# Fewer GpSimd additions in the last attention head, a later place in the queue for the first expert's weights, and a projection bias that GpSimd adds at the layer's start

## The reference

```
x = x + conv_attn(group_norm(x))      # 12 heads of 32 channels, 1024 x 1024 scores, with row and column biases by relative position
t = t + attn(layer_norm(t))           # 12 heads of 32 channels, the same 1024 tokens, plain scores
t = t + experts(layer_norm(t))        # 8 experts (384 -> 1536 -> 384), each token goes to its two best ones
# in each attention layer:
attn = softmax(q @ k.T * scale)       # per head
out  = (attn @ v) @ w_proj.T + b_proj
```

## Time and profile before

| | us |
|---|---|
| median of 3 runs | 1007.57 |
| the runs | 1009.1, 1007.57, 1000.21 |
| profiled execution, its time | 1002.1 |
| profiled execution, its span | 1000.3 |

### The profile page before, as it was taken

One profiled execution on the slowest core, in us unless ns is written; L12 is line 12 of the kernel. 1 busy time (PEld: TensorE's weight loads), 2 busy tenths in 40 slices (PEclk: granted clock), 3 DMA queues, 4 the chain that ended last, 5 costly groups with the idle time before them and its releaser, 6 DMA issues.

```text
span 1000.3 us, 17750 instructions
## 1 busy us (share of the span) xinstructions
PE 879.1 (88%) x6029; PEld 641.9 (64%) x6030; DVE 526.9 (53%) x883; ACT 328.3 (33%) x582; POOL 457.2 (46%) x360
## 2 busy tenths in 40 slices
PE   4969899999998899999898978616999999999991
PEld 3457466566665444555454534516999999999991
DVE  4334767676776444878788772722233333233224
ACT  0212144554545222445454544201222322322230
POOL 0000076676778200346464665558076177077303
PEclk9989699999999999999999989957999999999996
DMA  9564723534424019335464571351356455455214
GB/s 291 109 147 150 271 76 87 130 104 110 127 84 154 11 32 231 92 84 176 127 206 126 195 241 37 125 185 49 115 179 219 145 174 197 167 181 176 87 32 141
DMA packets 74367, 139.23 MB, mean 139 GB/s; under 512 B 11000, under 2 KB 49080, under 8 KB 74320
## 3 DMA queue, kind: packets, MB, share of 16 engines
q1 hardware_dynamic: 62720, 120.42, 39.3%
q10 hardware_dynamic: 9552, 11.93, 3.6%
q0 software_dynamic: 2048, 6.29, 2.0%
HBM read 91.39 MB, written 43.55 MB: 135 GB/s over the span
## 4 chain that ended last, share of the span: by engine, by line
PE 43%; issue 8%; DVE 8%; POOL 6%; DMA 3%; ACT 1%; DVEq 0%; SPq 0%; POOLq 0%; ACTq 0%
PE ps L796 14%; PE ps L807 11%; DVE mhalf L891 4%; PE ps L628 4%; PE ps L585 3%; PE ps L603 3%; POOL qf L518 3%; PE ps L727 2%; PE ps L618 2%; POOL xs L547 1%; POOL gy L556 1%; PE ps L683 1%; DVE rec L901 1%; PE ps L778 1%; ACT prob L1074 1%
## 5 line engine op out<-in xcount | busy, mean ns | idle before, releaser
L891 DVE TENSOR_REDUCE mhalf<-ps 128x1 f32<-128x512 f32 x384 | 242.0, 679 | 95.6 <-PE ps L603 94.1
L1074 ACT ACTIVATE prob<-ps 128x1024 f32<-128x1024 f32 x192 | 190.5, 1026 | 186.7 <-PE ps L628 110.0
L518 POOL TENSOR_TENSOR qf<-qf,prob 128x1024 f32<-128x1024 f32 x84 | 206.1, 2453 | 18.2 <-POOL qf L518 8.1
L796 PE MATMUL ps<-xT,w 128*128 128x128 f32 x1440 | 166.8, 278 | 1.6 <-ACT xT L1146 1.4
L796 PEld LDWEIGHTS ps<-xT,w 128*128 128x128 f32 x1440 | 166.1, 194 | 2.1 <-issue 2.1
L603 PE MATMUL ps<-km,qm 96*128 96x512 f32 x384 | 145.3, 445 | 20.1 <-DVE mhalf L891 15.3
L618 PE MATMUL ps<-qa,ka 97*128 97x512 f32 x384 | 147.4, 426 | 8.6 <-DMA qa<-row 8.2
L1163 ACT ACTIVATE h_f<-ps,b1c 128x128 f32<-128x128 f32 x240 | 68.4, 368 | 215.6 <-PE ps L796 161.0
L603 PEld LDWEIGHTS ps<-km,qm 96*128 96x128 f32 x384 | 74.1, 194 | 71.5 <-DVE mhalf L891 51.9
L514 POOL TENSOR_TENSOR qf<-prob 128x1024 f32<-128x1024 f32 x24 | 57.1, 2379 | 134.7 <-ACT prob L1074 134.7
L628 PE MATMUL ps<-prob,va 128*32 128x256 f32 x1536 | 109.8, 393 | 0.0
(11 more groups left out here) (130 smaller groups left out, 874.5 us busy)
## 6 DMA issues: line engine op xcount, KB each, us to landing
w<-in_w SPq DMA_DIRECT2D x24, 768.0 KB, 7.4
w_raw<-in_w SPq DMA_DIRECT2D x24, 768.0 KB, 12.0
heads<-parts SPq DMA_DIRECT2D x56, 256.0 KB, 4.7
qa<-heads SPq DMA_DIRECT2D x24, 256.0 KB, 3.7
ka<-heads SPq DMA_DIRECT2D x24, 256.0 KB, 3.9
qb<-heads SPq DMA_DIRECT2D x12, 512.0 KB, 5.1
xs<-zero SPq DMA_DIRECT2D x8, 768.0 KB, 4.9
qm<-heads SPq DMA_DIRECT2D x12, 384.0 KB, 3.7
```

Of the source, the lines that this page charges most:

```text
L518: pool.tensor_tensor(acc[b], acc[b], prob[:, n % NP, :], ALU.add).then_inc(a_ok[L], 1)
L796: last = mm(ps[:, g, c % HG * P:(c % HG + 1) * P], w1[b][:, k, c * P:(c + 1) * P], xT[:, k, :], start=(k == 0), stop=(k == KT - 1))
L891: v.tensor_reduce(mhalf[:, b, qt, half:half + 1], max_bank(qt, half), AX.X, ALU.max).then_inc(mx_ok[L], 1)
L1074: act.activation(prob[:, s % NP, :], ps[:, 2 + 2 * (s % 2):4 + 2 * (s % 2), :].rearrange("p a b -> p (a b)"), ACT.Exp).then_inc(p_ok[L], 1)
```

## The change

There are three edits.

1. In the last head of both layers GpSimd makes two additions (`ADDS_LAST` = 2) in place of five (layer 0) and four (layer 1). TensorE multiplies the tiles that are no longer added with ones: tiles 3, 4 and 5 in layer 0, tiles 3 and 4 in layer 1.
2. In layer 1 SP waits, ahead of the six loads of the first expert's weights, until TensorE has made the first scores of head 11. The stores of the heads 9, 10 and 11 stand behind these loads as before.
3. DVE's addition of the projection's bias (one instruction of 128 x 3072 a layer) is gone. GpSimd adds it in eight instructions of 128 x 384, ahead of its first work of the layer: in layer 0 when `t` and the constants have landed, in layer 1 when the normalisation at layer 0's end has read all of `t`.

```diff
--- before.py
+++ after.py
@@ -51,6 +51,7 @@
 BEHIND = 2
 RING = (0, 1, 7)
 ADDS = (5, 4)
+ADDS_LAST = 2
 
 
 SLOTS = (("Q_LO", "Q_HI", "RH_HI", "RW_HI", "RH_LO", "RW_LO", "K_HI", "K_LO"), ("Q_LO", "Q_HI", "K_HI", "K_LO"))
@@ -456,6 +457,7 @@
                 if L == 0:
                     load_wqkv(1)
                 else:
+                    sp.wait_ge(st_ok[1], TT * (NH - 1) + 1)
                     load_expert(sp, 0, 0)
                 for h in range(NH - 3, NH - 1):
                     store(h, h % 2, h)
@@ -502,7 +504,7 @@
 
             for L in L2:
                 def add_tiles(h, b, last=False):
-                    for n in range(1, ADDS[L] + 1):
+                    for n in range(1, (ADDS_LAST if last else ADDS[L]) + 1):
                         if n == 2 and not last:
                             take_v(h + 1, 1 - b)
                         pool.wait_ge(p_ok[L], TT * h + n + 1)
@@ -527,6 +529,13 @@
                     pool.sem_inc(pool_in, 1)
                     pool.tensor_copy(va[b][:], vf[:, :, cols]).then_inc(va_ok[L], 1)
 
+                if L == 0:
+                    pool.wait_ge(ld_c, 16 * 16)
+                    pool.wait_ge(ld_t, 16)
+                else:
+                    pool.wait_ge(tn_ok[0], TT)
+                for tt in range(TT):
+                    pool.tensor_tensor(t[:, tt, :], t[:, tt, :], bproj[:, L, :], ALU.add).then_inc(biased, 1)
                 take_v(0, 0)
                 add_tiles(0, 0)
                 add_tiles(1, 1)
@@ -629,22 +638,23 @@
                                   src[:, r * QUARTER:(r + 1) * QUARTER], start=start, stop=stop, skip_group_check=True)
                     return last
 
-                def out_product(h, b, s):
+                def out_product(h, b, s, adds=ADDS[L]):
                     pe.wait_ge(p_ok[L], TT * h + s + 1)
                     if s == 0:
                         wait(pe, vs_ok[L], h)
                         pe.wait_ge(va_ok[L], h + 1)
                     last = quarters(0, va[b][:, s, :], prob[:, s % NP, :], s == 0, s == TT - 1)
-                    if s > ADDS[L]:
+                    if s > adds:
 
                         last = quarters(1, ones[:, 0:HD], prob[:, s % NP, :], False, False)
                     last.then_inc(pv_ok[L], 1)
 
-                def sums(h, b):
-                    pe.wait_ge(a_ok[L], ADDS[L] * (h + 1))
+                def sums(h, b, adds=ADDS[L]):
+                    pe.wait_ge(a_ok[L], ADDS[L] * h + adds)
                     quarters(1, ones[:, 0:HD], acc[b], False, True).then_inc(s_ok[L], 1)
 
                 def head(h, b, first=False, left=2):
+                    adds = ADDS_LAST if left == 0 else ADDS[L]
                     for s in range(TT):
                         scores(h, b, s)
                         for later, qt in (MAXIMA_FIRST if first else MAXIMA)[s]:
@@ -653,7 +663,7 @@
                         if s % 2 == 1:
                             for done in (s - 1 - BEHIND, s - BEHIND):
                                 if done >= 0:
-                                    out_product(h, b, done)
+                                    out_product(h, b, done, adds)
                                 elif not first:
                                     out_product(h - 1, 1 - b, TT + done)
                         if s == BEHIND - 1 and not first:
@@ -718,8 +728,8 @@
                 head(NH - 2, 0, left=1)
                 head(NH - 1, 1, left=0)
                 for s in range(TT - BEHIND, TT):
-                    out_product(NH - 1, 1, s)
-                sums(NH - 1, 1)
+                    out_product(NH - 1, 1, s, ADDS_LAST)
+                sums(NH - 1, 1, ADDS_LAST)
 
 
                 def project(tt, ks):
@@ -931,15 +941,13 @@
                     for i in L2:
                         for rows in (slice(32, 64), slice(64, 96)):
                             v.memset(f(qm[i][rows, :]), 0.0).then_inc(wide_ok, 1)
-                    v.wait_ge(ld_t, 16)
-                v.tensor_tensor(t[:], t[:], bproj[:, L:L + 1, :].broadcast_to([P, TT, C]), ALU.add).then_inc(biased, 1)
                 head(NH - 1, 1, left=0)
                 for part in range(4):
                     invert_sums(NH - 1, part)
                 output(NH - 1, 1)
 
 
-                v.wait_ge(biased, L + 1)
+                v.wait_ge(biased, TT * (L + 1))
                 for tt in range(TT + 1):
                     if tt < TT:
                         v.wait_ge(pj_mm[L], tt + 1)
@@ -1069,7 +1077,7 @@
                         if s >= NP or not first:
                             last_h, last_s = (h, s - NP) if s >= NP else (h - 1, max(n for n in range(TT) if n % NP == s))
                             act.wait_ge(pv_ok[L], TT * last_h + last_s + 1)
-                            if last_s <= ADDS[L]:
+                            if last_s <= (ADDS_LAST if last and last_h is h else ADDS[L]):
                                 act.wait_ge(a_ok[L], ADDS[L] * last_h + max(last_s, 1))
                         act.activation(prob[:, s % NP, :], ps[:, 2 + 2 * (s % 2):4 + 2 * (s % 2), :].rearrange("p a b -> p (a b)"),
                                        ACT.Exp).then_inc(p_ok[L], 1)
```

## The result

Over 20 runs of each kernel the change takes 996.94 us where the kernel before takes 1003.2: a ratio of 0.9929 [0.991, 0.9949], by which the gain is 7.1 us. The forecast was 994 with a gain of 11.2. So the sign is right and the time lies in the range, but the gain stays under 1%, and four microseconds of it are missing. That 996.94 lies nearer to 994 than the gain does to 11.2 is luck: 994 stood for a kernel before of some 1005 us, and 20 runs put it at 1003.2. The profiled execution takes 995.97 us, with a span of 993.9.

The account below looks back on a forecast made before the run. The prediction took TensorE's chain as the bound, with four waits in the attention layers' last heads. Its terms, 2.88 + 0.37 + 6.02 + 1.03 + 0.89 = 11.2 us, gave 990.9 or 996.4, put midway at 994; range 987 to 1001.

Parts of the forecast that it names:

- The bias leaves VectorE: Head 10, both layers: without DVE's instruction GpSimd's long additions take 2.35 us; layer 0's whole wait of 2.88 us goes.
- the rival that the long additions have another cause: Head 10, both layers: GpSimd's 5.29 and 5.25 us stay, gain 5.4 us, about 999.5; chance 0.07.
- The moved bias is covered: Each layer's start: GpSimd's eight additions (8.4 us) beside DVE's splits cost 0, bounds 0 and 1.05 a layer.
- Layer 0: 3.25 forecast: Layer 0's last heads: 2.88 us from head 10's sums plus net 0.37 from fewer additions in head 11.
- The row and the sums of layer 1: Layer 1, heads 10 and 11: TensorE's 5.49 us wait for the row goes, head 10's sums come 6.02 us earlier.
- The rival of the late row: Layer 1: head 11's operands and projection weights still delay the row; gain 8.2 to 9.9 us, some 996; chance 0.2.
- no wait for it stands at TensorE: Layer 1, head 11: confirming sign that the row's load is issued by 591 and TensorE doesn't wait for the row.
- The stores behind the weights: Layer 1's end: head 9's store, behind the six loads, lands just in time for DVE; cost 0, bounds 0 and 2.
- DVE's last product waits for a DMA: Layer 1's end: sign that the prediction is wrong, DVE's product of head 11 held up by a DMA.
- The rival of a loss by late stores: Layer 1's end: stores land late behind the weights, a loss from 11.2 us late, 1011.5 at 150 GB/s; chance 0.03.
- The clock through layer 1's projection: Layer 1, last sums to first projection addition: full clock with both waits gone, 0.89 us won, bounds 0 and 0.89.

Follow-up runs that it names:

- second trace of before: The kernel before, unchanged, profiled once more: 1002.87 us.
- second trace: The changed kernel, unchanged, profiled once more: 997.52 us.
- weights last: Changed kernel with layer 1's six expert weight loads behind the stores of heads 9 to 11, without SP's wait: 0.9909 against the kernel before, 995.01 us.
- seven spare products: Changed kernel with seven more TensorE products, results unread, in the gaps of layer 1's projection: 0.9893 against the kernel before, 993.47 us.
- no wait of SP: Changed kernel with edit 2 undone, the expert's weights issued at once behind the projection weights: 0.9982 against the kernel before, 999.45 us.
- bias on VectorE: Changed kernel with edit 3 undone, VectorE adding the bias in one 128 x 3072 instruction: 0.9984 against the kernel before, 1001.38 us.
- edit 1 alone: Kernel before with only two GpSimd additions in the last head, bias and weights where they were: 0.9978 against the kernel before, 1006.09 us.
- all additions: Changed kernel with edit 1 undone, GpSimd making five and four additions in the last head: 0.9937 against the kernel before, 996.89 us.
- before with spare products: Kernel before with seven more TensorE products, results unread, in layer 1's projection: 1.0004 against the kernel before, 1006.66 us.

## Why the prediction was right in sign, and where it fell short

**The bias leaves VectorE: right.** The additions went from 5.29 and 5.25 to 2.38 us and came back with the instruction (5.30, 5.24), so the rival that the long additions have another cause falls. Undoing edit 3 costs 5.5 us by the ratios. One reading in the prediction is off by a little: the addition of layer 0 ended 313.31 + 5.29 = 318.60, that is 2.19 us after DVE's (316.41) and not 2.35. The Trainium skill ("SBUF — State Buffer", section "Who interferes with whom") has the two engines exclude each other when VectorE reads two SBUF inputs and GpSimd reads SBUF; these pairs of times agree with it.

**The moved bias is covered: right at 0.** Eight additions take 8.12 and 7.67 us (8.4 forecast). The split beside them is lengthened: its low half (line 883) from 1.23 to 1.90 us in layer 0, its high half (line 881) from 0.69 to 1.35 in layer 1. The next split idles 2.18 and 2.44 where it idled 3.13 and 3.09: the pause went into the cover.

**Layer 0: 3.25 forecast, 2.53 measured in this pair of traces.** The sums' waits went as forecast, but TensorE waited longer for the row (1.83 against 0.68). This wait had its row, and I took it for fixed. It isn't, and the change hasn't made it longer for certain: it is 1.37 in the second trace of before, and 0.26 to 1.88 in the changed kernels with the same layer 0. The second traces of before and after differ by 39.24 - 36.12 = 3.12 us, near the forecast.

**The row and the sums of layer 1: right.** From the first exponential of head 10 to its sums took 602.07 - 583.18 = 18.89 us and takes 589.19 - 576.30 = 12.89: 6.00, where 6.02 was forecast. To the last sums it is 7.58, where 6.02 + 1.03 = 7.05 was. What sets the time is GpSimd's addition, as forecast: it ends at 586.75 + 2.38 = 589.13, and the sums follow. TensorE's own way from the scores to the sums was mis-sized: at full clock it took 3.4 us (589.19 - 0.19 - 585.59) where the forecast had 2.7, so the wait there is 0.19 and not near 1. That the sum came out to 0.02 us owes something to luck.

The rival of the late row has little left: TensorE waits 0.35 and 0.69 us, though the sign "no wait for it stands at TensorE" failed. The row still needs 3.39 where a quiet queue gave 1.21. The rival named what is left of this: the projection weights ahead of the row. They are issued at 578.74 and land 5.1 us later, at 583.8, and the row's load is issued at 584.07. The same holds where the expert's weights come last of all (landed at 585.0, load issued at 585.18); it is not the six loads, which come after the row. The Trainium skill's rule ("DMA: Bandwidth & Descriptors", section "Queues, rings and completion order"), that each DMA engine takes its queues in turn, packet by packet, would let a 4 KB row through; no run shows that it did, for with the loads ahead of it the row took 5.31.

**The stores behind the weights: inside the bounds, at their upper half, and the sign that the prediction gave for being wrong.** I took 0 of 0 to 2. "DVE's last product waits for a DMA" came true: 1.55 us, and 1.26 in the second trace. From the last sums to the first addition layer 1 needs 608.19 - 599.28 = 8.91 us, layer 0 335.55 - 328.04 = 7.51; the clock is full in both, so the 0.89 of the clock term did come in that stretch, and the store's 1.40 took it away again. With the weights last it goes. The step that was mis-sized is the store's way behind the loads, 0.7 us in the forecast. The loads ran as taken (380 and 373 GB/s in the windows 588 to 594 and 594 to 600), but from 600 to 604 only 117 GB/s went through, and the store of 595.90 landed 8.0 us after its issue. The rival of a loss by late stores needed 11.2.

**The clock through layer 1's projection: the step that failed.** "With both gone I take full clock: 0.89", with bounds of 0 and 0.89, for the stretch up to the first addition; of the later stretches the text said that they could win or lose as much. Measured there: -6.59 to the scatter, -5.97 of it between the first and the last addition. In both traces of before, the clock fell when the last sums came after a wait of 1.89 us, and it was down for 3.4 us in the first part of the projection, where TensorE has nothing but products. Without that wait it doesn't fall there; it falls with the projection's first addition or soon behind it, where products, transposes and VectorE's normalisation take turns, and stays down for 17.1 us, and for 13.7 in the second trace. That the slow projection comes with edit 1 shows in the traces: seven of seven with it and without the seven spare products, none of three without it (17.37, 17.37, 17.86 us). A late store isn't needed: in four of the seven (weights last, no wait of SP, bias on VectorE, edit 1 alone) DVE waits for none. That the wait of 1.89 us was what held the fall in the cheap place is argued and not shown: with all additions, and before with spare products, the clock falls neither at the last sums nor in the projection.

The times show less than the traces. The spare products win nothing on the kernel before (1.0004) and give 0.9893 on the changed one, but that interval overlaps the change's (0.9862 to 0.9924, 0.991 to 0.9949). The mean granted clock over all runs speaks for them: 0.946 in the 20 runs after the change, 0.949 to 0.951 in the three changed kernels with seven spare products. Edit 1, forecast at 0.37 + 1.03 + 0.89 = 2.3 us, can't be sized: alone it has 0.9978 [0.9943, 1.0014], which holds both its forecast and nothing, and undone it leaves the time the same (0.9937).

**The sum.** Won at the ends 9.64 of 11.2 us, the 1.6 less being the row in layer 0 and the store; lost in the projection 6.59 in this execution; won elsewhere 3.3, most of it by the number of falls in the heads of layer 1, which differs from run to run of one kernel. By the ratios the loss is less than in the trace: the spare products win 0.36%, 3.6 us, which would be most of the four that are missing; as the intervals overlap, this size is likely and not shown. The edits don't add up one by one either: undoing the second or the third costs 5.3 to 5.5 us each, more together than the gain, since the sums of head 10 need both. The forecast said so, but called them "the first and the third"; edit 1 has no part in head 10.

**Open.** Why the clock falls where it does is not settled. The kernel with all additions has waits of 1.18 and 0.98 us at the end of layer 1 and holds full clock, the one with the weights last has 0.54 at the same place as the 0.98 and falls. Why it stays down so long with TensorE busy again isn't settled either, nor why the heads of layer 1 have one fall in one execution and five in another.

## What to carry to other kernels

When a wait is taken away, look at the granted clock in the stretch behind it, and give the clock a term there as wide as the whole stretch at half speed: here it was 6.59 us in one trace, where the forecast had at most 0.89. Where products alternate with short gaps, a few spare ones that nobody reads can be cheaper than the gaps: with seven of them the clock stayed at 1.00 here in three kernels of three, and by the ratios they were worth some 3.6 us, though the intervals overlap. When loads are moved behind a small urgent transfer, look at what stands behind them on their queue: here DVE waited 1.55 us for a store, for the buffer that it frees. And before two traces are compared stretch by stretch, count the falls of the clock in each: one more of them cost about 1.5 us in a stretch that the change had no part in.

## What I had not expected of the hardware

The granted clock stayed at 0.50 for 17.1 us (608.2 to 625.3) though TensorE was busy 0.95 to 1.00 of every window of 1 us from 614 on; the falls in the heads last 3.4 us each. And a row of 4 KB on ScalarE's queue took 4.7 to 5.7 us from issue to issue with large loads on SP's queue beside it (five traces), 2.4 to 3.7 with only the projection weights ahead of it (eight traces), and 1.2 where these had been issued 4.1 us before it or the queues were quiet. In the eight, its load was issued within 0.5 us of the landing of the projection weights: a small transfer on one queue came through here about when the large one issued before it on the other landed.
